# First folded keys in the first dispatch, the second half's statistics first, the last gathers in pairs

## The chip, the cores and the metric

The kernel runs on one core of a Trainium2 chip. The metric is the device time of one execution in microseconds (us), as the median of several runs. TensorE (PE) multiplies matrices from SBUF into PSUM banks, VectorE (DVE) and ScalarE (ACT) work on tiles, GpSimd (POOL) computes and issues indirect DMAs, and SyncE (SP) issues the plain DMAs. Each engine runs its own program in order and waits on semaphores.

## The reference

`x` is [16, 128, 128] in float32, and the context is [16, 77, 96]. Four layers follow each other, and each adds a gated cross-attention to the context and then a gated feed-forward part:

```
layer 0: 16 heads x 8  on the context;  FFN: top 2 of 8 experts, gelu, 128-512-128
layer 1: 16 heads x 64 on the context;  FFN: dense mixture of 8 experts, 128-128
layer 2: 1 head x 128  on the context;  FFN: top 1 of 8 experts, silu, 128-512-128
layer 3: 16 heads x 8  on the context;  FFN: ternary weights, gelu, layernorm
attention: out = softmax(q k^T * scale) v @ Wo
```

In layer 1 the key is `context @ Wk` and the query `x @ Wq`, so the scores of a head are `x (Wq_h Wk_h^T) context^T`. The product in the brackets doesn't depend on the data.

## The kernel before

The program of every engine is written out by hand, with waits on counted semaphores, and goes through the stages in this order: `heads8(0)` (attention of layer 0), `experts(0)`, `heads64` (attention of layer 1), the dense mixture, `head128`, `experts(1)`, `heads8(1)`, the ternary layer. The batches 0 to 15 come in four groups of four (GB = 4), and a group is normalised by `front_a` (statistics, DVE), `rsqrt_front` (POOL) and `front_b` (DVE).

**Experts.** `experts(run)` takes the 2048 tokens in two halves, hh = 2*run and 2*run + 1. For a half, PE transposes (`turn`, L1377) and makes the gate logits (`logits`, L1387), DVE picks the experts (`route`), PE counts (`ranks`, L1396), and DVE computes each token's row (`slots`). POOL scatters the normalised rows to `xs` in DRAM by 16 (top 2) or 8 (top 1) indirect DMAs (`spread`, L701). SP loads them again (L453), and PE works off 23 or 15 tiles per half: `turn_slots` (L1429), up (L1439), and down (L1455). DVE copies each input (`take`, L2206 or L2203) and each output (`give`, L2216), SP stores outputs to `ys` (L502), POOL gathers them (`collect`, L715), and DVE adds them to `x` (`combine`, L2231). The second layer's bias goes to `x` through PE (`second_bias` L1409, `add_bias` L1418) and DVE (`bias8`, L2128). `stats8`, `variance8` (L1993) and `norm8` on DVE, with `token_roots` on POOL between them, normalise a half. `weigh` computes the gate weights. The second half's routing is done in the gap in which the first half's rows go to DRAM and back, and its scatter goes beside the first half's tiles.

**heads64.** `folded_weights` (PE L1505) multiplies Wq and Wk of each head, ACT and DVE split the products into `l1w` high and low parts, and `folded_keys` multiplies them by a group's context, three matmuls for each of 16 heads (L1123 to L1125), with copies to `k1` by ACT and DVE. Before, the products are made inside the second half of `experts(0)`, and the first group's keys at the start of `heads64`. `own_values` makes the values, and `scores` (L1554), exps on ACT (L825) and sums follow batch by batch.

**heads8.** The queries and keys are computed on PE for a group, split, stored to DRAM by SP (`store_queries` L417, `store_keys` L397) and loaded back in another layout (`query_roles` L428, `key_roles` L408). POOL multiplies each batch's keys by a mask (`keys`, L606), and PE makes scores (L1231), exps on ACT, sums (L1265) and products with the values (L1276). In `heads8(1)` SP's order for g = 1, 2, 3 is: for g >= 2 `key_roles(1, g)`, for g = 2 also `store_keys(1, 3)`; `store_queries(1, g)`; `query_roles(1, g)`; and after g = 1 a wait until the feed-forward part of layer 2 has been added to all of `x` ("ff", counted by `combine`), then the loads of the ternary weights (L568 to L570). The gathers and the combination of the very last half, hh = 3, stand in `heads8(1)`: POOL's `collect(3)` at b = 0, DVE's `last_rows` at b = 2.

## Time and profile before

| | us |
|---|---|
| median of 3 runs | 780.34 (780.26 to 781.79) |
| the profiled execution | 786.76 |
| its span in the trace | 784.7 |
| PE busy | 669.0 (85%) |
| DVE busy | 454.6 (58%) |
| ACT busy | 395.8 (50%) |
| POOL busy | 311.4 (40%) |
| mean granted TensorE clock | 0.921 |

The span is the time from the first to the last instruction in the trace. A granted clock of 1.00 is 2.4 GHz, and 0.50 is 1.2 GHz. In the timelines a row has the start, the busy time, the engine and line, the operation and how many instructions it merges; in brackets is the engine's idle time before it, and what ended that. `SPq` is SP issuing a DMA, not the DMA's own time.

### The profile page before, as it was taken

Reading aid. Unit: us, or ns where it says so; the run is one execution under the profiler, and the core shown is the slowest. Engines: PE = TensorE matmul, PEld = TensorE weight load, DVE = VectorE, ACT = ScalarE, POOL = GpSimd, SP = SyncE. Lnnn points to the kernel's source line nnn. Section 1 sums busy time; section 2 is a strip of 40 time slices with the busy share of each in tenths; the row PEclk is TensorE's granted clock in tenths of the full one; section 3 lists DMA queues with packets and bytes.
Section 4 is the critical chain, followed back from the end, with each engine's and each line's share of the span. In section 5 each row is a group of like instructions: output and inputs, shape, how many; then the busy total and the mean of one; then the engine's idle time right before and its main releaser. Section 6 shows DMA issues by size and latency. Waiting matters only on the chain.

```text
span 784.7 us, 17363 instructions
## 1 busy us (share of the span) xinstructions
PE 669.0 (85%) x6445; PEld 557.1 (71%) x6445; DVE 454.6 (58%) x1408; ACT 395.8 (50%) x969; POOL 311.4 (40%) x266
## 2 busy tenths in 40 slices
PE   3799995589999799899998999884699868999894
PEld 3587773379999778688786854563589756777784
DVE  5375768533224668666675667755433334778783
ACT  4475542145566366365665666421155744666471
POOL 4654431725143338123141337502224446545032
PEclk9998998579999999999999999995599987999997
DMA  6543751866775301000000020003357553331001
GB/s 171 153 117 67 209 169 38 257 165 177 230 207 148 88 15 34 1 1 2 1 1 1 2 80 2 1 1 96 110 136 225 162 161 96 115 75 42 3 15 41
DMA packets 60717, 70.93 MB, mean 90 GB/s; under 512 B 7051, under 2 KB 40859, under 8 KB 60635
## 3 DMA queue, kind: packets, MB, share of 16 engines
q1 hardware_dynamic: 57563, 63.52, 28.7%
q0 software_dynamic: 3072, 6.30, 2.7%
q8 instruction: 54, 0.88, 0.5%
q14 instruction: 28, 0.23, 0.1%
HBM read 48.89 MB, written 20.91 MB: 89 GB/s over the span
## 4 chain that ended last, share of the span: by engine, by line
PE 67%; DVE 17%; issue 5%; DMA 4%; ACT 3%; SPq 2%; POOL 1%; POOLq 0%; ACTq 0%; DVEq 0%
PE banks L1439 8%; PE banks L1455 7%; PE banks L1554 4%; PE banks L1276 4%; PE banks L1253 4%; PE banks L1165 3%; PE banks L1563 3%; PE banks L1574 3%; PE banks L1123 3%; PE banks L1231 3%; PE banks L1125 3%; PE banks L1124 3%; PE banks L1265 3%; PE banks L1607 2%; DVE rr L1901 2%
## 5 line engine op out<-in xcount | busy, mean ns | idle before, releaser
L962 ACT ACTIVATE hT<-banks,wup 128x128 f32<-128x128 f32 x304 | 86.5, 368 | 74.4 <-PE banks L1439 60.0
L893 ACT ACTIVATE pT<-banks 77x512 f32<-77x512 f32 x128 | 69.2, 590 | 58.8 <-PE banks L1253 56.8
L1439 PE MATMUL banks<-xTs,wup 128*128 128x128 f32 x608 | 85.0, 286 | 3.2 <-issue 3.2
L701 POOL DMA_INDIRECT xs<-xn,slot x48 | 46.8, 974 | 102.1 <-DVE ysb L2216 52.2
L606 POOL TENSOR_TENSOR kbd<-k,const 96x1248 fp32r<-96x1248 f32 x32 | 72.8, 2285 | 32.6 <-PE banks L1253 30.1
L661 POOL TENSOR_TENSOR sh<-sh,rd 128x616 f32<-128x616 f32 x32 | 38.9, 1216 | 112.1 <-DVE rd L1858 111.8
L1439 PEld LDWEIGHTS banks<-xTs,wup 128*128 128x128 f32 x608 | 78.4, 202 | 4.5 <-issue 4.2
L1455 PE MATMUL banks<-wd,hT 128*128 x608 | 80.8, 277 | 0.3
L2216 DVE COPY ysb<-banks 128x128 f32<-128x128 f32 x76 | 22.1, 291 | 91.9 <-PE banks L1455 82.8
L1455 PEld LDWEIGHTS banks<-wd,hT 128*128 128x128 f32 x608 | 73.8, 192 | 1.1 <-issue 0.8
L586 POOL TENSOR_TENSOR rstd<-vv,const 128x4 f32<-128x4 f32 x24 | 25.4, 1060 | 115.8 <-DVE vv L1805 115.5
L715 POOL DMA_INDIRECT back<-ys,slot x48 | 46.4, 966 | 53.5 <-DMA ys<-ysb 26.8
L1895 DVE TENSOR_REDUCE nm<-banks 128x8 f32<-128x616 f32 x64 | 50.9, 796 | 27.5 <-PE banks L1231 25.2
L825 ACT ACTIVATE sh<-sh 128x308 f32<-128x308 f32 x64 | 27.1, 460 | 43.7 <-DVE sh L1848 42.5
L1901 DVE RECIPROCAL rr<-banks 128x128 f32<-128x128 f32 x32 | 30.6, 956 | 24.2 <-PE banks L1276 24.1
L1253 PEld LDWEIGHTS banks<-q,kbd 128*77 128x77 f32 x448 | 41.6, 156 | 1.9 <-ACT q L800 1.8
L1253 PE MATMUL banks<-q,kbd 128*77 128x128 f32 x448 | 42.3, 240 | 0.6 <-ACT q L800 0.4
L1276 PE MATMUL banks<-pT,vp 128*32 128x128 f32 x1024 | 41.6, 284 | 0.0
L1231 PE MATMUL banks<-kbd,q 96*128 96x312 f32 x112 | 32.6, 375 | 8.4 <-DVE nm L1895 5.7
L1827 DVE SCALAR_TENSOR_TENSOR x<-banks,tg,x 128x128 f32<-128x128 f32 x48 | 16.7, 348 | 38.1 <-PE banks L1574 22.0
L1265 PE MATMUL banks<-pT,const 128*32 128x128 f32 x1024 | 36.3, 280 | 2.2 <-issue 1.5
L800 ACT ACTIVATE prob<-banks 77x512 f32<-77x512 f32 x64 | 33.6, 585 | 8.8 <-PE banks L1165 8.8
(323 smaller groups left out, 1570.7 us busy)
## 6 DMA issues: line engine op xcount, KB each, us to landing
wup<-in_up SPq DMA_DIRECT2D x76, 258.0 KB
q<-queries SPq DMA_DIRECT2D x21, 256.0 KB, 4.3
queries<-qc SPq DMA_DIRECT2D x8, 512.0 KB
wd<-in_down SPq DMA_DIRECT2D x8, 512.0 KB
ys<-ysb SPq DMA_DIRECT2D x16, 256.0 KB
k<-keys SPq DMA_DIRECT2D x24, 156.0 KB, 3.6
xs<-zt SPq DMA_DIRECT2D x2, 1472.0 KB, 10.7
keys<-kc SPq DMA_DIRECT2D x8, 312.0 KB
```

What stands on the lines that cost most here:

```text
L606: pool.tensor_tensor(kbd[b % NB8][0:96, :, :, :].bitcast(F32R), kb, m, ALU.mult).then_inc(h8.kbd, 1)
L701: pool.indirect_dma_start(xs[hh], bass.IndirectOffsetOnAxis(ap=idx[hh % 2][k_][:, t:t + 1], axis=0), xn8[hh % 2][:, t, :], None).then_inc( ...
L715: pool.indirect_dma_start(back[:, k_, t, :], None, ys[hh], bass.IndirectOffsetOnAxis(ap=idx[hh % 2][k_][:, t:t + 1], axis=0))\
L893: act.activation(pT[b % 2][0:SK, u, :], ps[0:SK, 2 + u % 2, :], ACT.Exp, scale=D8 ** -0.5)\
L962: ins = act.activation(hT[T % 3][:, c, :], ps[:, T % 2, c * P:c * P + P], func, bias=wup[T % NW][:, HID + c:HID + c + 1])
L1231: ins = pe.matmul(ps[:, i, 0:HG * SP], q_[0:96, 2 * pair + i, b % GB, :].bitcast(F32R), kbd[b % NB8][0:96, 2 * pair + i, :, :].rearrange(" ...
L1253: ins = pe.matmul(ps[0:SK, 2 + u % 2, j * P:j * P + P], kbd[b % NB8][:, u, j, 0:SK].bitcast(F32R), q_[:, u, b % GB, :].bitcast(F32R), star ...
L1265: pe.matmul(ps[32 * j:32 * j + 32, 4 + b % 2, P:2 * P], const[:, C_PAD + 32 * u:C_PAD + 32 * u + 32], pT[b % 2][:, u, j * P:j * P + P], st ...
L1276: ins = pe.matmul(ps[32 * j:32 * j + 32, 4 + b % 2, 0:P], vp[b // GB % 2][:, at:at + 32], pT[b % 2][:, u, j * P:j * P + P], start=(u == 0) ...
L1439: ins = pe.matmul(ps[:, T % 2, c * P:c * P + P], w_[:, c * P:c * P + P], xTs[T % 3][:, :], start=True, stop=True)
L1455: ins = pe.matmul(ps[:, 6 + T % 2, 0:P], hT[T % 3][:, c, :], wd[:, bass.ds(expert, 1), c * P:c * P + P].rearrange("p o n -> p (o n)"), sta ...
L1895: dve.tensor_reduce(m_, s_, AX.X, ALU.max, negate=True).then_inc(h8.max, 1)
```

## The change

The products of the layer 1 weights and the first group's 16 folded keys are made in the first gap of `experts(0)`. The weights wqT and wkT get a place of their own and are loaded earlier by SP, the keys go to a new tile `k1_first`, and ACT alone copies them. `folded_keys(0, ...)` is gone at the start of `heads64` on PE, ACT and DVE. There PE makes the first four value products right after `front`, and ACT copies them ahead of its first exps. In both runs of `experts` DVE makes the second half's statistics first, PE does `turn` and `logits` ahead of the bias, `bias8(hh, 0)` comes after the second half's routing, and `bias8(hh, 1)` in the first tile. POOL computes `token_roots(1)` after one scatter instead of three, and `token_roots(3)` ahead of the scatters. At the end of the second half of `experts(0)`, `combine`, `front_a` and `front_b` come a tile earlier. In `heads8(1)` `collect(3)` is cut in four pairs of gathers, with the masked keys of batch 3 behind the first, and `last_rows` is cut in two, at b = 2 and b = 5.

```diff
@@ -462,8 +479,6 @@
                     resident(6, 8)
-                    sp.dma_start(wqT[:, :, :], a["wqT"]).then_inc(ld.l1raw, 16)
-                    sp.dma_start(wkT, a["wkT"]).then_inc(ld.l1raw, 16)
...
@@ -536,6 +551,9 @@
                 query_roles(0, g)
+            sp.wait_ge(ld.xrest, 16)
+            sp.dma_start(wqT[:, :, :], a["wqT"]).then_inc(ld.xrest, 16)
+            sp.dma_start(wkT[:, :, :], a["wkT"]).then_inc(ld.xrest, 16)
...
@@ -624,7 +642,7 @@
                 for b in range(B):
-                    if b + 2 < B and (b or run == 0):
+                    if b + 2 < B and (b >= 2 or run == 0):
...
@@ -633,7 +651,11 @@
                         if run:
-                            collect(3)
+                            collect(3, 0, 4)
+                            keys(1, 3)
+                            collect(3, 1, 4)
+                    if run and b in (2, 3):
+                        collect(3, b, 4)
...
@@ -690,8 +712,8 @@
                         m = k_ * HT + t
-                        if hh % 2 == 0 and m == 3:
-                            token_roots(hh + 1)
+                        if hh == 0 and m == 1:
+                            token_roots(1)
...
@@ -764,6 +786,7 @@
             token_roots(2)
+            token_roots(3)
...
@@ -827,6 +850,8 @@
                         outputs(G, i - 2)
+                    if i == 0 and G == 0:
+                        value_copies(0, 0)
...
@@ -951,6 +976,18 @@
+            def folded_weights_hi():
+                for j in range(4):
+                    act.wait_ge(h64.qmm, j // 2 + 1)
+                    copy(folded(0, j), ps[0:DC, 4 * (j // 2) + j % 2, :].rearrange("p (c d) -> p c d", c=4)).then_inc(su.hi, 1)
+            def first_keys():
+                for h in range(H):
+                    act.wait_ge(h64.kmm, h + 1)
+                    copy(k1_first[:, h, :, :].rearrange("p b t -> p (b t)"), ps[:, first_bank(h), 0:GB * SP]).then_inc(h64.q, 1)
...
@@ -965,17 +1002,17 @@
                     tanh(2)
+                else:
+                    folded_weights_hi()
...
                 turned(2 * run + 1, 1)
+                if run == 0:
+                    first_keys()
...
                         hidden(BASE[hh] + i)
-                        if hh == 1 and i in (5, 6, 12, 13):
-                            j = (5, 6, 12, 13).index(i)
-                            act.wait_ge(h64.qmm, j // 2 + 1)
-                            copy(folded(0, j), ps[0:DC, 2 + j % 2, :].rearrange("p (c d) -> p c d", c=4)).then_inc(su.hi, 1)
...
@@ -996,13 +1033,19 @@
-                def own_values(g, part):
+                def value_copies(g, part):
...
                              ps[0:SK, 2 + i % 4, :]).then_inc(h64.v, 1)
+                def own_values(g, part):
+                    if g or part:
+                        value_copies(g, part)
...
@@ -1012,14 +1055,12 @@
-                folded_keys(0, 0)
-                folded_keys(0, 1)
...
                 for g in range(0, NG - 1):
-                    attend(h64, g, D64 ** -0.5, outputs, own_values)
+                    attend(h64, g, D64 ** -0.5, outputs, own_values, value_copies)
...
                 gate_exp(0)
-                attend(h64, NG - 1, D64 ** -0.5, outputs, own_values)
+                attend(h64, NG - 1, D64 ** -0.5, outputs, own_values, value_copies)
...
@@ -1458,12 +1499,21 @@
                 hh = 2 * run
-                second_bias(hh)
-                add_bias(hh)
+                if run == 0:
+                    folded_weights(0)
+                    folded_weights(1)
...
                 logits(hh + 1)
+                second_bias(hh)
+                if run == 0:
+                    first_keys(range(0, 8))
                 ranks(hh + 1)
+                if run == 0:
+                    first_keys(range(8, H))
+                add_bias(hh)
+                if run == 0:
+                    pe.wait_ge(h64.q, H)
...
@@ -1488,21 +1538,25 @@
                             add_bias(hh + 1)
-                        if hh == 1 and i in (3, 10):
-                            folded_weights(i // 10)
...
+            def first_keys(units):
+                ct = tuple(c_[0:DC, 0:GB, :].rearrange("p b t -> p (b t)") for c_ in (chi, clo))
+                pe.wait_ge(su.lo, 2 * NG)
+                for h in units:
+                    if h >= 4:
+                        pe.wait_ge(h64.q, h - 3)
+                    split3(ps[:, first_bank(h), 0:GB * SP],
+                           tuple(w_[0:DC, h // 8, (h % 8) * P:(h % 8) * P + P] for w_ in l1w), ct).then_inc(h64.kmm, 1)
...
-                pe.wait_ge(ld.l1raw, 64)
-                if j == 0:
-                    pe.wait_ge(mo.xb, 4)
-                else:
-                    pe.wait_ge(su.lo, NG + 2)
+                pe.wait_ge(ld.xrest, 48)
...
                     at = h % 8 // 2 * P
-                    ins = pe.matmul(ps[0:DC, 2 + h % 2, at:at + P], wkT[rows, h // 2, :], wqT[rows, h // 2, :],
+                    ins = pe.matmul(ps[0:DC, 4 * j + h % 2, at:at + P], wkT[rows, h // 2, :], wqT[rows, h // 2, :],
...
@@ -1515,24 +1569,31 @@
                     for h in range(8 * part, 8 * part + 8):
-                        if h % 8 >= 4:
-                            pe.wait_ge(h64.q if h % 2 else h64.k, 8 * g + h // 2 - 1)
-                        elif g:
+                        if h % 8 >= 4 and h % 2:
+                            pe.wait_ge(h64.q, by_act(g, h // 2 - 1))
+                        elif h % 8 >= 4:
+                            pe.wait_ge(h64.k, by_dve(g, h // 2 - 1))
+                        else:
                             pe.wait_ge(h64.v, 8 * g - 7 + 4 * part + h % 8)
-                        elif part:
-                            pe.wait_ge(h64.q if h % 2 else h64.k, h // 2 - 1)
...
-                def own_values(g, part):
+                def value_units(g, part):
...
                     for i in range(4 * part, 4 * part + 4):
-                        if i >= 4 and g < NG - 1:
-                            pe.wait_ge(h64.q if i % 2 else h64.k, 8 * (g + 1) + i // 2 + 1)
+                        if i >= 4 and g < NG - 1 and i % 2:
+                            pe.wait_ge(h64.q, by_act(g + 1, i // 2 + 1))
+                        elif i >= 4 and g < NG - 1:
+                            pe.wait_ge(h64.k, by_dve(g + 1, i // 2 + 1))
...
                                tuple(w_[0:DC, 2, 512 * (i % 2):512 * (i % 2) + 512] for w_ in l1w)).then_inc(h64.vmm, 1)
+                def own_values(g, part):
+                    if g or part:
+                        value_units(g, part)
...
@@ -1540,19 +1601,19 @@
                     if b == 0 and u == 0:
-                        pe.wait_ge(h64.k, 8 * g + 8)
-                        pe.wait_ge(h64.q, 8 * g + 8)
+                        pe.wait_ge(h64.k, by_dve(g, 8))
+                        pe.wait_ge(h64.q, by_act(g, 8 if g else H))
...
                         if g < NG - 1:
-                            pe.wait_ge(h64.k, 8 * g + 16)
-                            pe.wait_ge(h64.q, 8 * g + 16)
+                            pe.wait_ge(h64.k, by_dve(g + 1, 8))
+                            pe.wait_ge(h64.q, by_act(g + 1, 8))
...
                     return pe.matmul(ps[:, u % 2, 0:4 * SP].rearrange("p (h t) -> p h t", h=4),
-                                     xT[(g + 2 * NG) % 2][:, b * P:b * P + P], k1[g % 2][:, 4 * u:4 * u + 4, b, :],
+                                     xT[(g + 2 * NG) % 2][:, b * P:b * P + P], folded_rows(g)[:, 4 * u:4 * u + 4, b, :],
...
@@ -1568,15 +1629,14 @@
                 def project(g, b):
-                    pe.wait_ge(ld.l1raw, 96)
+                    pe.wait_ge(ld.l1raw, 64)
...
-                folded_keys(0, 0)
-                folded_keys(0, 1)
                 front(2 * NG)
+                value_units(0, 0)
...
@@ -1942,7 +2002,10 @@
                     if b == 2 and between:
-                        between()
+                        between((0,), (0,))
+                        lk.wait()
+                    if b == 5 and between:
+                        between((0,), (1,))
...
@@ -2177,21 +2240,26 @@
                 hh = 2 * run
+                wait_done(dve, "h1" if run else "h8", 1)
+                stats8(hh + 1, 0)
+                stats8(hh + 1, 1)
+                variance8(hh + 1)
...
                     slots(hh)
-                wait_done(dve, "h1" if run else "h8", 1)
-                stats8(hh + 1, 0)
-                stats8(hh + 1, 1)
-                variance8(hh + 1)
-                weigh(hh, gate)
-                bias8(hh, 0)
+                else:
+                    weigh(hh, gate)
...
                 norm8(hh + 1, 1)
-                bias8(hh, 1)
+                if run:
+                    weigh(hh, gate)
+                if run == 0:
+                    for j in range(4):
+                        folded_weights_lo(j)
...
                     route(hh + 1, part)
+                bias8(hh, 0)
...
@@ -2248,6 +2316,7 @@
                             if i == 0:
+                                bias8(hh, 1)
...
@@ -2256,18 +2325,16 @@
                                 combine(hh - 1, 0, i - 10)
-                            if run == 0 and i in (7, 8, 14, 15):
-                                folded_weights_lo((7, 8, 14, 15).index(i))
-                            if run == 0 and i in (19, 20):
-                                combine(hh - 1, 1, i - 19)
+                            if run == 0 and i in (18, 19):
+                                combine(hh - 1, 1, i - 18)
...
                                 key_lo(1, i - 3)
-                            if run == 0 and i == nt - 2:
+                            if run == 0 and i == nt - 3:
...
                                 front_a(0, n)
-                            if run == 0 and i == nt - 1:
+                            if run == 0 and i == nt - 2:
...
```

## Rows read from the trace of the kernel before

**Rows 1.** The page: which engine's work the chain that ended last was.

```profile
PE 67%; DVE 17%; issue 5%; DMA 4%; ACT 3%; SPq 2%; POOL 1%; POOLq 0%; ACTq 0%; DVEq 0%
```

**Rows 2.** Windows: stretch, length, busy PE, PEld, DVE, ACT, POOL, clock, DMA share, GB/s.

```profile
160.00:166.00 6.00, 5.30 (x24) 4.90 (x25) 1.09 (x4) 1.82 (x7) 0.00 (x0) 0.51 0.81 210
...
265.00:270.00 5.00, 5.00 (x27) 5.00 (x26) 1.93 (x4) 1.55 (x4) 3.54 (x5) 0.68 0.31 105
```

**Rows 3.** Timeline of POOL at the first dispatch: start, us, work, idle before.

```profile
132.90 1.24 POOL L701 DMA_INDIRECT xs<-xn,slot  x1 [23.43 <-DVE slot L2109]
...
155.42 0.96 POOL L701 DMA_INDIRECT xs<-xn,slot  x1 [0.30 <-issue]
```

**Rows 4.** Timeline of PE at the first dispatch and the first tiles.

```profile
160.53 0.69 PE L1429 MATMUL banks<-const,xsb 128*128 128x128 f32 x2 [4.67 <-DMA xsb<-xs]
...
161.66 3.62 PE L1439 MATMUL banks<-xTs,wup 128*128 128x128 f32 x16
...
169.35 1.13 PE L1439 MATMUL banks<-xTs,wup 128*128 128x128 f32 x8
```

**Rows 5.** Timeline of DVE at the first dispatch and the first tiles.

```profile
135.45 0.17 DVE L1993 TENSOR_REDUCE vv<-mv 128x8 f32<-128x16 f32 x1
...
168.96 0.28 DVE L2206 COPY xTs<-banks 128x128 f32<-128x128 f32 x1
...
179.59 1.27 DVE L2128 TENSOR_TENSOR x<-x,banks 128x512 f32<-128x512 f32 x2
```

**Rows 6.** Windows of line 1505 alone: stretch, length, PE, PEld, clock, DMA, GB/s.

```profile
215.00:259.00 44.00, 2.23 (x32) 1.80 (x32) 1.00 0.59 170
```

**Rows 7.** Timeline of PE at the start of heads64.

```profile
260.57 0.41 PE L1123 MATMUL banks<-chi,l1w_hi 96*128 96x312 f32 x1 [1.42 <-DVE ysb L2216]
...
271.25 0.60 PE L1134 MATMUL banks<-const,xn 128*128 128x128 f32 x4
272.62 1.29 PE L1554 MATMUL banks<-k,xT_even 128*128 128x312 f32 x4 [0.78 <-ACT xT_even L800]
```

**Rows 8.** Timelines of SP, ACT and POOL around the start of heads64.

```profile
214.92 0.38 SPq L502 DMA_DIRECT2D ys<-ysb  x1
...
218.70 0.98 POOL L715 DMA_INDIRECT back<-ys,slot  x1 [17.60 <-DMA ys<-ysb]
...
248.27 12.63 SPq L502 DMA_DIRECT2D ys<-ysb  x3
...
272.50 1.28 ACT L825 ACT_TABLE_LOAD   x1
```

**Rows 9.** Timeline of PE at the second dispatch (experts(1)).

```profile
549.50 3.77 PE L1418 MATMUL banks<-b2m,cT 32*128 32x512 f32 x4 [0.51 <-DVE cT L2122]
...
555.95 3.58 PE L1387 MATMUL banks<-rraw,xT 128*128 128x8 f32 x16 [0.78 <-ACT xT L800]
...
566.48 0.47 PE L1429 MATMUL banks<-const,xsb 128*128 128x128 f32 x1 [2.65 <-DVE xTs L2203]
```

**Rows 10.** Chain that ended last, at the start of heads8(1): start, us, what.

```profile
635.10 3.85 DMA queries<-qc
...
639.85 4.97 DMA q_first<-queries
```

**Rows 11.** Timelines of DVE, SP and PE in heads8(1).

```profile
666.94 2.18 DVE L2231 SCALAR_TENSOR_TENSOR x<-back,share,x 128x128 f32<-128x128 f32 x8
...
673.91 0.36 SPq L568 DMA_DIRECT2D wfr<-in_fc  x1
...
676.74 0.38 SPq L397 DMA_DIRECT2D keys<-kc  x1
...
680.59 0.34 SPq L417 DMA_DIRECT2D queries<-qc  x1
...
685.79 0.96 DVE L1901 RECIPROCAL rr<-banks 128x128 f32<-128x128 f32 x1 [1.19 <-PE banks L1276]
...
691.24 0.50 PE L1231 MATMUL banks<-kbd,q 96*128 96x312 f32 x2
```

27 lines of the change are left out of this document (16 added, 11 removed).

## The prediction

> **What bounds the kernel now.** I first read the chain of work that ended last. PE holds 67% of it [rows 1], so anything that only lightens DVE, ACT or POOL is worth nothing, and a gap of PE is worth its full length. Then I followed PE's timeline to the places that the diff touches and looked for the wait that ends last. There are five. At the first dispatch PE waits 4.67 us for the first rows from DRAM, and its first 16 up products take 3.62 us, while 8 of them take 1.13 us later [rows 4]: the granted clock is 0.51 in that stretch [rows 2]. The second half of `experts(0)` is tile after tile of PE work, with the weights' products in it [rows 6]. At the start of `heads64` PE makes keys from 260.57 to 271.25, with only a little else to do [rows 7]. At the second dispatch the first up product waits for DVE, which is still in the second half's `slots` [rows 9]. In `heads8(1)` PE is fed by queries that go to DRAM and back [rows 10, 11].
>
> **1. The first keys leave heads64.** PE's last output is copied out at about 260.5, and `front` starts at 271.25 [rows 7]; the 10.7 us between are 16 keys. All of it goes if nothing else is late. Two things are. `front_b` now comes before DVE's last `give` and PE's transposes start about 1.0 us later than the keys did. The value copies now stand on ACT ahead of the first exps and wait until the last outputs have landed in `ys`: SP ends issuing them at 248.27 + 12.63 = 260.9 [rows 8]. An earlier output store was issued at 214.92, and the gather that waited for it began at 218.70 [rows 8], so about 3.8 us; that gives some 264.7 and with issue gaps 265.6. Then come the copies and a table load of 1.28 us [rows 8]. Old first scores at 272.62 become 262.9 or so, but the first exps are held for about 1.2 us more. I take **-8.5** (bounds -7, both waits in full, and -10.7, none). The copies also fill the idle time of ACT, so they cost nothing later.
>
> **2. Products out of the second half.** 16 products of two forms took 2.23 us of PE at full clock [rows 6], and that stretch has no PE gap that they could have filled: **-2.2**. The same work in the gap of the first dispatch has 4.67 us of idle PE and more before it [rows 4].
>
> **3. The chain to the first rows (run 0).** The first load waits for POOL's 16 scatters, which run back to back from 132.90 to 156.38 [rows 3]. `token_roots(1)` moves from before the fourth to before the second scatter. POOL gets there at 134.14, but its input is written by DVE until 135.62 [rows 5]. Every later scatter is behind this wait in POOL's order: 135.62 - 134.14, with a semaphore's way, **+1.6**. Its bounds: 0, if DVE's earlier statistics (they no longer wait behind anything but the last addition to `x`) come sooner; +3, if PE instead sets the end. PE now has 48 key products before `turn_slots`: the 16 keys took 10.7 us at the start of `heads64` [rows 7], where the clock was at 0.68 for part of the way [rows 2], so I take 12.5 us as the most at the low clock throughout; with turns, logits, counts and a bias product of 3.8 us [rows 9] PE would be ready at about 163.4 against 160.53 [rows 4]. In the first half of the gap PE has work without a pause, and I expect it done by 162.
>
> **4. bias8(0, 1) in the first tile.** Its two halves of DVE work take 1.27 us in another tile [rows 5]. In tile 0 DVE's copy at 168.96 to 169.24 is what PE's product at 169.35 waits for [rows 4, 5], so there is no slack: **+1.3**. In run 1 the same happens: **+1.3**. What hid it before was the gap.
>
> **5. The second dispatch.** Before: bias product 549.50 to 553.27, turns, logits to 559.5, route, ranks, `slots`, take, up [rows 9]; the end is DVE's. Now the statistics are there before `slots(2)` ends, and turns and logits come ahead of the bias product: its 3.77 us and some 3 us of statistics and weights go out of the way, logits end at about 552.6 and `slots(3)`, which ended about 6.6 us behind them, at 559.2. Then PE is the last: ranks at 555.9, bias product to 560.3, `turn_slots`, take and up at 561.2 instead of 566.95. `token_roots(3)` is ahead of the scatters now (POOL was idle there), so the rows are there by 558.6. **-5.7** (bounds -4 and -6.5).
>
> **6. heads8(1), b = 2.** `combine` takes 2.18 us for eight additions [rows 11], and PE waited for the DVE work behind it. Half of it goes to b = 5, where DVE has 1.19 us of idle time [rows 11]: **-1.1**.
>
> **7. heads8(1), SP.** "ff" now means b = 5 of DVE: the work ahead of the new half ends at 685.79 - 1.19 = 684.60 [rows 11], minus the 1.1 of part 6, plus the 1.1 of the half itself, so 684.6. SP waits there in its order for g = 1, and behind it are three loads of ternary weights, `key_roles(1, 2)` (three), `store_keys(1, 3)` and then `store_queries(1, 2)`, which before was issued at 680.59 [rows 11], when its data came. Issuing these (seven, without the last) took from 673.91 to 677.12 before, 3.2 us [rows 11], so the store goes at about 687.95. A store and a load in sequence took 3.85 + 0.9 + 4.97 = 9.7 us at the start of the stage [rows 10], and I allow for 0.8 us less. So the queries of batch 8 are there at 696.7 to 697.7; PE needs them at 691.24 - 1.1 = 690.1 [rows 11]. That is a gap of 6.6 to 7.6 us, and PE comes out of it at a low clock as at the first dispatch [rows 2], for 1.5 to 2 us; some 0.8 us of small DVE waits of that stretch are absorbed. **+8** (bounds +4, if only part of the load is waited for, and +9).
>
> What the change moves at the end of `experts(0)` (`combine`, `front_a`, `front_b` a tile earlier) costs nothing: DVE has idle time before every output copy, and if that were gone it would cost up to 1.1 us, one combination.
>
> **Sum.** -8.5 - 2.2 + 1.6 + 1.3 - 5.7 + 1.3 - 1.1 + 8 = -5.3 us, on a span of 784.7 us in an execution of 786.76 us. The median of the runs shown is 780.34; the profiled one is 0.8% longer, and I take the difference over as it is: **775.0 us**.
>
> **What the Trainium skill adds.** The low clock at the first tiles is shown by the rows. Its page "TensorE: Matmul & The Clock Gate", section "What's actually happening", says that "the default state is throttled, and activity releases the throttle". By that the key products in the gap would be of use twice: the first 16 up products would take about 1.8 us instead of 3.62, and that is rival B. Its page "DMA: Bandwidth & Descriptors", section "Rules for kernel authors", tells the author to issue a DMA early and to wait late. Part 7 does the reverse with SP, and by the fit of the page's section "Anatomy of one DMA — SWDGE (gpsimd) path", 2.0 us plus the bytes by 436 GB/s, an estimate of store and load is 4 + 2.9 = 6.9 us for 0.5 and 0.77 MB. By that the term 7 would be about 2.5 us smaller. The rows have 9.7 for the two [rows 10], and I go by them.
>
> **Rivals.**
> A (forecast): **775.0**, within 771.5 to 778. Chance 0.45.
> B: the gap's key products keep PE busy and the tiles start at the full clock. For it: the clock fell only where PE idled. Against it: PE idles 4.67 us for the rows anyway. The first 16 and next 8 products would be some 2.5 us shorter, and a `heads8(1)` gap of only 4 us (a store right behind "ff") would give 4 more: 775.0 - 2.5 - 4 = **768.5**, or either one, to 772. Chance 0.25.
> D: the wait at the start of `heads64` takes the place of the one removed. ACT stands still for the last `ys` store with the exps queued behind it, and DVE and PE wait for the exps. The first exps were at 273.8 and would be at 269 or later: -4.5 instead of -8.5, **779.0** (778 to 780). For it: SP issued those stores until 260.9 [rows 8], when PE was through with the tiles. Chance 0.17.
> C, slower than before: the SP wait is dearer. Place: from "ff" to the first scores of batch 8. The query store stands behind six loads of weights and keys, and all share the DMA engines; the store and load could take 14 us instead of 9.3, and the batches after the gap run at half the clock for the 5.5 us that the first tiles needed [rows 2, 4], 2.7 us more. Price +16 instead of +8: **783.0**. It decides from a delay of 15 us on, since the other terms sum to -13.3. For it: nothing else on SP can go around the wait. Against: these loads are small. Masked keys on POOL, now queued behind the gathers, would add to it if they became late. Chance 0.13.
> That the change doesn't do what it says (keys in the gap push `turn_slots` out by as much as they save) is inside the +3 of part 3, since 160.53 to 163.4 is much less than 10.7.
>
> **How the numbers follow.** The forecast is that of A. The range of 768.5 to 780.0 leaves out C and a little of B's end. About 0.2%, 1.6 us, is what a measurement of this kernel can tell from no change: faster is at or under 778.8, with A, B and a third of D, 0.76; within 0.2% is the rest of D, 0.11; slower is C, 0.13.
>
> **What would show it.** Right: no L1123 products after the last tile; first scores near 263 and exps before 270; first up product of run 0 near 162 and of run 1 near 561; `store_queries` of group 2 near 688 less the shift, with a gap of PE of 6 to 8 us before the first scores of batch 8. Wrong: a first up product of run 0 after 165 (PE bound), a DVE gap behind the value copies of over 4 us, or no gap of PE at batch 8, which alone would make it 767.

## The result and the profile after

The changed kernel takes **776.63 us** (median of 20 runs, 773.57 to 783.96), the kernel before 780.51 (20 runs, 778.23 to 783.11). The ratio is 0.9958 [0.9939, 0.9977]: 0.42% faster, 3.3 us (3.9 us by the medians; the interval is 1.8 to 4.8). The forecast was 775.0 in a range of 768.5 to 780.0. The profiled execution took 774.30 us with a span of 772.1, 2.3 below its median, while the profiled one of before was 6.3 above the median of 780.51. So the two traces differ by 12.6 us, and most of what that has over 3.3 is a difference of executions. I therefore read stages, each against traces of other kernels that have the same code in that stage. The traces start at different offsets, so times are compared from one milestone to the next, and not as they stand.

The page's chain, to hold against [rows 1]:

```profile
PE 65%; DVE 17%; DMA 6%; issue 4%; ACT 3%; POOL 3%; SPq 1%; POOLq 0%; ACTq 0%; DVEq 0%
```

DMA and POOL have gained on the chain, PE has lost. The four places follow, each as the timeline of one engine. First PE at the first dispatch:

```profile
153.85 1.98 PE L1459 MATMUL banks<-b2m,cT 32*128 32x512 f32 x4
160.02 0.66 PE L1470 MATMUL banks<-const,xsb 128*128 128x128 f32 x2 [4.19 <-DMA xsb<-xs]
161.12 3.62 PE L1480 MATMUL banks<-xTs,wup 128*128 128x128 f32 x16
170.45 1.13 PE L1480 MATMUL banks<-xTs,wup 128*128 128x128 f32 x8 [1.03 <-issue]
```

The keys are in the gap and PE still waits 4.19 us for the first rows (4.67 in [rows 4]); the 16 up products still take 3.62 us. The windows of PE show why (stretch, length, PE busy, clock, DMA share, GB/s):

```profile
149.00:156.00 7.00, 6.64 (x36) 0.99 0.15 49
156.00:160.00 4.00, 0.00 (x0) 0.50 0.45 103
160.00:164.00 4.00, 3.81 (x17) 0.50 0.95 277
```

The granted clock was 0.99 while PE worked and 0.50 after it had stopped. It was also 0.50 in the windows 144 to 146 and 146 to 148, with PE busy with keys for all of the 4 us: these keys were themselves made at half the clock. POOL, which sends the rows, has a new wait ahead of its second scatter (`token_roots`, L629), and the last of the 16 scatters starts 24.23 us after the first, 22.52 in the kernel before [rows 3]:

```profile
130.57 1.24 POOL L723 DMA_INDIRECT xs<-xn,slot  x1 [23.41 <-DVE slot L2172]
133.38 1.67 POOL L629 TENSOR_TENSOR rstd<-vv,const 128x8 f32<-128x8 f32 x1 [1.57 <-DVE vv L2056]
...
154.80 0.96 POOL L723 DMA_INDIRECT xs<-xn,slot  x1 [0.30 <-issue]
```

At PE's fourth tile there is a new wait of 1.03 us, and DVE's timeline has what held it: `bias8(0, 1)` and, behind it, the gate weights of `weigh` (seven small operations, of which the first is shown) ahead of the copy that PE needs:

```profile
167.67 1.27 DVE L2191 TENSOR_TENSOR x<-x,banks 128x512 f32<-128x512 f32 x2
168.86 0.16 DVE L2112 TENSOR_SCALAR rs<-rs 128x8 f32<-128x8 f32 x1
...
170.07 0.28 DVE L2274 COPY xTs<-banks 128x128 f32<-128x128 f32 x1
```

Next the start of `heads64`, PE, then ACT:

```profile
259.21 0.66 PE L1175 MATMUL banks<-const,xn 128*128 128x128 f32 x4 [1.58 <-DVE ysb L2284]
262.50 1.22 PE L1615 MATMUL banks<-k_first,xT_even 128*128 128x312 f32 x4
```

```profile
261.35 2.04 ACT L823 ACTIVATE v<-banks 77x512 f32<-77x512 f32 x4 [0.84 <-DMA ys<-ysb]
263.41 1.28 ACT L848 ACT_TABLE_LOAD   x1
264.70 0.81 ACT L848 ACTIVATE sh<-sh 128x308 f32<-128x308 f32 x2
```

No key product stands between the last output copy and `front` (10.7 us in [rows 7]). The wait for `ys` is there, but costs ACT 0.84 us, and the table load runs beside the DVE subtraction (L1908, from 264.14) whose result the exps need anyway: the first exps start at 264.70, 2.20 us behind the first scores. In the kernel before they stood 2.23 us behind them, and waited for that subtraction, not for the table load, which ended at 273.78:

```profile
274.85 0.85 ACT L825 ACTIVATE sh<-sh 128x308 f32<-128x308 f32 x2 [1.07 <-DVE sh L1848]
```

At the second dispatch, PE (to hold against [rows 9]):

```profile
545.33 3.78 PE L1459 MATMUL banks<-b2m,cT 32*128 32x512 f32 x4
...
550.22 3.62 PE L1480 MATMUL banks<-xTs,wup 128*128 128x128 f32 x16
```

The bias product is now the last thing before the tiles, and nothing is waited for behind it. Last `heads8(1)`: DVE's half combination, SP and PE:

```profile
662.37 1.13 DVE L2299 SCALAR_TENSOR_TENSOR x<-back,share,x 128x128 f32<-128x128 f32 x4
```

```profile
663.53 0.36 SPq L586 DMA_DIRECT2D wfr<-in_fc  x1
...
664.94 2.31 SPq L425 DMA_DIRECT2D k<-keys  x3
...
667.83 0.38 SPq L434 DMA_DIRECT2D queries<-qc  x1
```

```profile
678.10 0.89 PE L1272 MATMUL banks<-kbd,q 96*128 96x312 f32 x2 [8.84 <-DMA q<-queries]
```

The second half of the additions ends at 663.50 and SP goes on at 663.53: the wait of part 7 of the forecast. The query store stands six DMAs behind it, and PE idles 8.84 us for what it brings. The page's chain goes through exactly these loads, with 4.25 us for the store's DMA and 5.06 for the load behind it (3.85 and 4.97 in [rows 10]).

### The profile page after: what moved, and what is told of

Its sections match the earlier page's. It is cut to its first block, busy times and chain, and to the rows that moved or that the text cites. A ratio compares the mean times of both kernels' runs of the same rounds, so it can differ in the third digit from the quotient of the medians.

```text
span 772.1 us, 17362 instructions
## 1 busy us (share of the span) xinstructions
PE 665.8 (86%) x6445; PEld 557.5 (72%) x6445; DVE 452.2 (59%) x1400; ACT 399.3 (52%) x977; POOL 312.1 (40%) x266
## 4 chain that ended last, share of the span: by engine, by line
PE 65%; DVE 17%; DMA 6%; issue 4%; ACT 3%; POOL 3%; SPq 1%; POOLq 0%; ACTq 0%; DVEq 0%
PE banks L1480 9%; PE banks L1496 7%; PE banks L1615 4%; PE banks L1294 3%; PE banks L1317 3%; PE banks L1206 3%; PE banks L1624 3%; PE banks L1635 3%; PE banks L1272 3%; PE banks L1164 3%; PE banks L1165 3%; PE banks L1166 2%; PE banks L1306 2%; PE banks L1667 2%; DVE rr L1961 2%
## 6 DMA issues: line engine op xcount, KB each, us to landing
xs<-zt SPq DMA_DIRECT2D x2, 1472.0 KB, 12.6
```

## The stages of every kernel

Below is the time between milestones of PE's timeline, in us: the last row of scores of `heads8(0)` to the first transposed rows (**dispatch**), to the end of the tiles of run 0, to the first scores of `heads64` (**start**), to `head128`'s last product with `b_raw`, its last queries (**attention**), to the first up product of run 1 (**dispatch 2**), to the end of its tiles (**tiles 2**). The stretch from there to the first scores of `heads8(1)` is left out (8.3 to 9.8 us). **End** goes from those scores to PE's last product, and 9.9 us follow it in every trace.

| | dispatch | tiles | start | attention | dispatch 2 | tiles 2 | end |
|---|---|---|---|---|---|---|---|
| before | 42.91 | 98.63 | 13.46 | 243.68 | 50.45 | 69.66 | 129.65 |
| after | 44.73 | 97.62 | 4.86 | 242.41 | 45.31 | 69.29 | 134.36 |
| e1_sp_late | 44.90 | 97.10 | 6.30 | 242.38 | 44.03 | 70.52 | 126.32 |
| e3_after_no_pairs | 44.52 | 97.69 | 4.73 | 242.49 | 45.32 | 71.30 | 127.33 |
| e2_before_pairs_split | 42.97 | 97.48 | 13.39 | 243.60 | 50.37 | 68.80 | 137.87 |
| e4_before_split | 42.80 | 97.68 | 13.38 | 243.67 | 50.11 | 67.91 | 135.59 |
| e5_before_keys3_first | 43.03 | 97.91 | 13.41 | 243.54 | 49.92 | 68.01 | 131.16 |
| e8_after_run1_old | 45.72 | 98.00 | 4.73 | 242.51 | 49.76 | 68.13 | 136.40 |
| e6_bias_gap | 44.78 | 95.81 | 4.85 | 240.81 | 44.54 | 67.75 | 125.68 |
| e7_warm | 44.45 | 94.81 | 4.61 | 242.34 | 45.26 | 67.68 | 127.79 |
| e12_keys_11 | 44.73 | 97.04 | 6.28 | 242.49 | 44.07 | 66.92 | 126.39 |
| e9_roots_m3 | 48.11 | 98.41 | 4.71 | 242.35 | 45.32 | 69.32 | 130.53 |
| e10_roots_warm | 53.42 | 96.00 | 4.68 | 242.45 | 44.19 | 68.73 | 132.03 |
| e11_keys_again | 48.28 | 98.75 | 13.12 | 241.40 | 44.44 | 68.84 | 130.29 |

Up to `heads8(1)` the code of before stands in four traces (before, e2, e4, e5) and that of after in three (after, e1, e3). Among them dispatch and attention repeat to within 0.4 us; start and dispatch 2 differ by up to 1.6 and 1.3 us, tiles 2 by 2.0. In the start of e1 and e12 the four value products of PE ran at half the clock (0.50 and 0.55 in the windows from 260 to 262, 1.00 in the changed kernel), and this is their 1.5 us. So one trace is enough for terms of several us, and for none of one. The trace of e6 is of an execution 4.7 us under its median, the fastest of six.

## The experiments

**SP's order in heads8(1), from the changed kernel.** The theory was that the loss of 8 us comes from the wait alone: put it and the ternary loads behind the queries of g = 2.

```diff
 # e1_sp_late
-                if g == 1:
+                if g == 2:
...
-                    if run and b in (6, 10, 11, 12, 14):
-                        ternary_weights((6, 10, 11, 12, 14).index(b))
+                    if run and b in (7, 10, 11, 12, 14):
+                        ternary_weights((7, 10, 11, 12, 14).index(b))
```

> The changed kernel, but SP waits for ff and loads the ternary weights only after the queries of group 2 (store_queries(1, 2), query_roles(1, 2)), and DVE's first ternary step moves from b = 6 to b = 7. Theory (SP's order makes the 8.84 us gap of PE before batch 8): the gap is gone, with the low clock after it, the span is 8 to 10 us shorter than that of the changed kernel, about 768 us, 0.984 of before. Rival (the late ff costs the time wherever it stands: the ternary loads are then late for DVE and POOL at b = 6 and 7): the gap only moves one or two batches on, and the time stays within 3 us of the changed kernel, 774 to 777.

Measured: 768.38 us, ratio 0.9844 [0.9819, 0.9869]: 8.2 us under the changed kernel by the medians, 8.9 by the ratios (1.14%). The stage end is 8.0 shorter. SP, and PE's scores of batch 8:

```profile
660.44 0.34 SPq L434 DMA_DIRECT2D queries<-qc  x1
...
667.54 0.36 SPq L586 DMA_DIRECT2D wfr<-in_fc  x1
```

```profile
672.90 0.50 PE L1272 MATMUL banks<-kbd,q 96*128 96x312 f32 x2
```

The store goes before the ternary loads, the scores of batch 8 wait for nothing, and in PE's stretch from 668 to 676 (669 to 678 is the gap of the changed kernel) 6.90 of 8.00 us are busy at a clock of 1.00. Beside SP's wait and the loads behind it only DVE's first ternary step moved, by one batch, since it reads what they load: the place of the wait is the cause.

**The same edits in the kernel before.** If that is so, the later half of the last combination alone must make the kernel before slower. e4 cuts `last_rows` in two; e2 also has the gathers in pairs.

```diff
 # e4_before_split
-                        between()
+                        between((0,), (0,))
+                        lk.wait()
+                    if b == 5 and between:
+                        between((0,), (1,))
 # e2_before_pairs_split: as e4, and
-                    if b + 2 < B and (b or run == 0):
+                    if b + 2 < B and (b >= 2 or run == 0):
...
-                            collect(3)
+                            collect(3, 0, 4)
+                            keys(1, 3)
+                            collect(3, 1, 4)
+                    if run and b in (2, 3):
+                        collect(3, b, 4)
```

> The kernel before with the edits in heads8(1) alone: gathers in pairs, keys(1, 3) behind the first pair, last_rows at b = 2 and b = 5. Theory: batches 0 to 3 gain about 4 us and the gap before batch 8 costs 8 to 9, so about 4.5 us slower than before, 785 us, 1.006. Rival (the edits are a gain, and the gap seen in the changed kernel's trace comes from its other parts): 776 to 777 us, 0.995.

> The kernel before with one edit: the last combination cut in two, at b = 2 and b = 5, gathers as before. Theory: the gap before batch 8 alone, +8 to +9, less 1.1 for the half that leaves b = 2: 787 to 788 us, 1.009. Rival (the gap needs the pairs too, since their last gathers make ff late): within 1.5 us of before.

Measured: e4 789.38, ratio 1.0106 [1.0083, 1.0129]; e2 790.25, 1.0124 [1.0099, 1.0149]. PE in e4:

```profile
691.31 0.89 PE L1231 MATMUL banks<-kbd,q 96*128 96x312 f32 x2 [8.66 <-DMA q<-queries]
```

The gap of the changed kernel stands there (8.83 us in e2), and the split alone brings it: +8.3 us against the 781.04 of the kernel before, measured beside it, and +9.2 with the pairs, with intervals that overlap. For e4 I had expected 787 to 788, for e2 785, which was too low: the gain of 4 us in the first batches didn't come.

**The changed kernel without them.** e3 has `collect(3)`, the masked keys and `last_rows` as before, and all else changed.

```diff
 # e3_after_no_pairs
-                            collect(3, 0, 4)
-                            keys(1, 3)
-                            collect(3, 1, 4)
-                    if run and b in (2, 3):
-                        collect(3, b, 4)
+                            collect(3)
...
-                        between((0,), (0,))
-                        lk.wait()
-                    if b == 5 and between:
-                        between((0,), (1,))
+                        between()
```

> The changed kernel with heads8(1) as before: eight gathers in a row, last_rows whole at b = 2. Theory: 4.5 us faster than the changed kernel, about 772 us, 0.989 of before, and no gap of PE before batch 8. Rival (pairs help): 3 to 4 us slower than the changed kernel, 780 us.

Measured: 769.86 us, ratio 0.9854 [0.983, 0.9878]. The parts outside `heads8(1)` are worth 11.4 us (1.46% of 780.51), and those inside cost 0.9958 / 0.9854 = +1.06%, 8.2 us, with some 2.4 us of uncertainty from the two intervals. I had expected 4.5 us for them.

**Masked keys ahead of the gathers.** One piece of the change seemed harmless or good: POOL makes batch 3's keys before most gathers.

```diff
 # e5_before_keys3_first
-                    if b + 2 < B and (b or run == 0):
+                    if b + 2 < B and (b >= 2 or run == 0):
...
-                            collect(3)
+                            collect(3, 0, 4)
+                            keys(1, 3)
+                            for part in range(1, 4):
+                                collect(3, part, 4)
```

> The kernel before with one edit: in heads8(1) the masked keys of batch 3 come behind the first two gathers instead of behind all eight; the combination stays whole at b = 2. Theory: PE's wait for these keys goes (0.71 us in the trace of e4_before_split), 0.5 to 1 us of gain, time within 0.2% of before. Rival (the gathers ahead of the keys are what made the start of heads8(1) 3.8 us longer in the trace of before than in that of the changed kernel): 3 to 4 us faster, 0.995.

Measured: 784.64, ratio 1.0048 [1.0025, 1.007], some 3.8 us slower; theory and rival were both wrong. POOL, then DVE:

```profile
651.56 2.26 POOL L606 TENSOR_TENSOR kbd<-k,const 96x1248 fp32r<-96x1248 f32 x1 [3.84 <-PE banks L1256]
...
660.26 0.94 POOL L718 DMA_INDIRECT back<-ys,slot  x1 [0.30 <-issue]
661.22 1.29 POOL L622 TENSOR_TENSOR x<-x,a_raw 128x512 f32<-128x512 f32 x1
662.45 2.27 POOL L606 TENSOR_TENSOR kbd<-k,const 96x1248 fp32r<-96x1248 f32 x1
```

```profile
660.67 6.05 DVE L2234 SCALAR_TENSOR_TENSOR x<-back,share,x 128x128 f32<-128x128 f32 x8
```

The keys wait 3.84 us for PE and push the six gathers behind them. The last one is issued at 660.26, and the eight additions then fall beside two POOL products of 1.29 and 2.27 us: they take 6.05 us instead of 2.18 [rows 11]. PE's next scores came after 1.99 us of idle time. The excess of 3.87 us on DVE is of the size of the 3.8, but no run removes the overlap alone, so this cause is argued and not shown.

**The tile-0 stall.** e6 is e1 with `bias8(0, 1)` and the gate weights in the gap of run 0, and `weigh` a tile later in run 1.

```diff
 # e6_bias_gap: as e1, and after slots(hh + 1)
+                if run == 0:
+                    bias8(hh, 1)
+                    weigh(hh + 1, gate)
...
-                            if i == 0:
+                            if i == 0 and run:
                                 bias8(hh, 1)
+                            if i == 1 and run:
```

> e1_sp_late with the bias additions and the weights of the second half moved out of tile 0: in run 0 into DVE's idle time behind slots(1), in run 1 the weights from tile 0 to tile 1. Theory (term 4: 1.3 us in each run, and the weights' share of the stall too): up product of the fourth tile 8.8 us or less behind the first transposes in run 0, and 1 to 1.5 us sooner in run 1, 2 to 3 us in all, 766 us. Rival (DVE's stall in tile 0 is made up by later tiles, which wait for ACT and loads anyway): no gain.

Measured: 765.48, ratio 0.9813 [0.9777, 0.9848]. The totals of e6 and e1 can't be told apart by their intervals, so the expected gain of 2 to 3 us isn't shown; the stage can be told apart. PE in e6, the first transposes and the fourth tile:

```profile
160.91 0.66 PE L1470 MATMUL banks<-const,xsb 128*128 128x128 f32 x2 [4.25 <-DMA xsb<-xs]
...
169.56 1.06 PE L1480 MATMUL banks<-xTs,wup 128*128 128x128 f32 x8
```

That is 8.65 us from the one to the other, 8.82 in the kernel before [rows 4], and 160.02 to 170.45, 10.43, in the changed kernel. The wait of 1.02 to 1.03 us at the fourth tile stands in all four traces with that code (the changed kernel, e1, e3, e8) and in none of those without it (e6, e7, e12).

**Rival B by itself: PE kept busy.** e7 is e6 with transposes that nobody reads, 32 in the first gap, 12 and 8 around the turns of the second.

```diff
 # e7_warm: as e6, and
+                def warm(n):
+                    for _ in range(n):
+                        pe.transpose(ps[:, 0, 0:P], idn, idn)
...
+                else:
+                    warm(12)
...
+                else:
+                    warm(8)
...
+                    warm(32)
```

> e6_bias_gap with transposes of a constant that nobody reads, in PE's waits: 32 in run 0 between the bias product and the first rows, and 12 and 8 in run 1 around the logits. Theory (the first tiles are slow only because PE idled before them): granted clock near 1.00 from the first tile on in run 0, its first 16 up products in 1.8 us instead of 3.62, 2 to 2.5 us less in run 0, and 0 to 3 less in run 1. Rival (the clock comes up too late whatever PE did before, or the first rows and weights bound these tiles): 3.62 us again and no gain, or a loss by the transposes that run late.

Measured: 764.87, ratio 0.9802 [0.9769, 0.9836]. PE and its windows in run 0:

```profile
156.99 3.71 PE L1449 MATMUL banks<-const 128*128 128x128 f32 x32
161.27 0.44 PE L1475 MATMUL banks<-const,xsb 128*128 128x128 f32 x2 [0.56 <-DMA xsb<-xs]
162.15 1.96 PE L1485 MATMUL banks<-xTs,wup 128*128 128x128 f32 x16
```

```profile
156.00:160.00 4.00, 4.00 (x31) 1.00 0.18 56
160.00:164.00 4.00, 3.16 (x27) 1.00 0.91 255
```

With the gap filled the clock is 1.00 and the 16 products take 1.96 us instead of 3.62. The tiles are 1.0 us shorter than e6's; in the whole time that isn't measurable. Run 1 stayed at 3.62, so the 20 fillers there gave nothing.

**The second dispatch.** e8 has run 1's order on DVE and PE, and `token_roots(3)`, as before.

```diff
 # e8_after_run1_old (core)
+                if run:
+                    second_bias(hh)
+                    add_bias(hh)
...
+                if run:
+                    for part in range(4):
+                        route(hh, part)
+                    slots(hh)
```

> The changed kernel with the order of the second dispatch as before (statistics behind slots(2), bias products ahead of the turns and logits, bias additions ahead of the tiles, token_roots(3) among the scatters). Theory: the first up product of run 1 comes 5.7 us later and tile 0 is 1.3 us shorter, so 4 to 4.5 us slower than the changed kernel, 781 us, 1.001 of before. Rival (the gain was run-to-run variation of the profiles): within 1.5 us of the changed kernel.

Measured: 780.8, ratio 1.0007 [0.9981, 1.0033], beside 0.9958 for the changed kernel. The stage is back at 49.76 us, and the first up product waits for DVE as in [rows 9]:

```profile
557.38 0.48 PE L1471 MATMUL banks<-const,xsb 128*128 128x128 f32 x1 [2.64 <-DVE xTs L2278]
557.65 3.62 PE L1481 MATMUL banks<-xTs,wup 128*128 128x128 f32 x16
```

**POOL's roots late again, and fillers.** e9 is e6 with `token_roots(1)` before the fourth scatter; e10 adds 24 unread transposes to it.

```diff
 # e9_roots_m3: as e6, and
-                        if hh == 0 and m == 1:
+                        if hh == 0 and m == 3:
 # e10_roots_warm: as e9, and after the keys, in run 0
+                    warm(24)
```

> e6_bias_gap with token_roots(1) behind the third scatter again, as in the kernel before. Theory (term 3: POOL waits 1.57 us for the variance, and every scatter behind it is late by that): the first transposes of run 0 come 1.5 to 1.9 us sooner, 43.0 us after the last scores of heads8(0) instead of 44.8, and the span is 1.5 us shorter, 764 us. Rival (the later norm8(1) makes turns, logits and keys late, and PE or DVE then sets the first tile): no gain or a loss of up to 1 us.

> e9_roots_m3 with 24 transposes of a constant, read by nobody, between the bias product and the first rows of run 0 alone. Theory: the first 16 up products take 1.9 to 2.0 us instead of 3.62, as in e7_warm, 1 to 2 us less than e9_roots_m3, 762.5 us. Rival (what the clock gives is taken by the next wait, for DVE's input copies and the weights' loads): within 0.5 us of e9_roots_m3.

Measured: e9 774.27, 0.9855 [0.9817, 0.9892]; e10 777.77, 0.9887 [0.9843, 0.993], both measured beside a kernel before that took 784.55. Both missed. POOL did what e9's theory said: the last scatter starts 22.64 us after the first, as in the kernel before (24.24 in e6). But PE came later. In e9, at the end of the dispatch:

```profile
160.05 3.78 PE L1459 MATMUL banks<-b2m,cT 32*128 32x512 f32 x4
163.76 0.69 PE L1470 MATMUL banks<-const,xsb 128*128 128x128 f32 x2
```

The bias product that ended at 155.8 in the changed kernel ends at 163.8, at half the clock, and the transposes follow it with no wait: the rows are no longer what comes last. Ahead of it ACT and DVE stood still together, and PE idled 2.83 us before 156.03 (one row of each of the two):

```profile
155.54 0.43 ACT L823 ACTIVATE k_first<-banks 128x312 f32<-128x312 f32 x1 [3.09 <-remote]
```

```profile
156.28 0.23 DVE L2153 TENSOR_TENSOR plan<-banks,const 128x64 f32<-128x64 f32 x1 [4.94 <-remote]
```

With PE as the bound, e10's fillers delay the tiles by their full length, and in this execution they began at the low clock, 24 of them in 5.38 us where e7 had 32 in 3.71:

```profile
164.48 5.38 PE L1449 MATMUL banks<-const 128*128 128x128 f32 x24
```

Behind them the first 16 up products took 1.95 us instead of 3.62, as the theory said, and the tiles 96.00 instead of 98.41: 2.4 us back for 5.3 us paid. So these two say nothing, by their times, on what the earlier `token_roots` costs.

**The keys put back.** e11 is e6 with 48 unread key products before `front` of `heads64`, on PE alone.

```diff
 # e11_keys_again: as e6, and in heads64
+                for h in range(H):
+                    split3(ps[:, 2 + h % 2, 0:GB * SP],
+                           tuple(w_[0:DC, h // 8, (h % 8) * P:(h % 8) * P + P] for w_ in l1w), ct)
```

> e6_bias_gap with 48 matmuls of the size of the first keys put again at the start of heads64 on PE, ahead of front; nobody reads them and nobody copies them. Theory (PE's work between the last tile and the first scores sets that stretch, term 1): 48 by 0.143 us is 6.9 us, less 1.5 us in which PE waited there anyway, so the first scores come 5.4 us later and the time is 5 to 7 us up, 771 us. Rival (the copies of the keys by ACT and DVE, or the wait for the last stores, made the old stretch long): under 2 us.

Measured: 782.75, beside e9 and e10, 0.9972 [0.9949, 0.9996]. Against its own base e6 (0.9813, measured at another time) that is +1.6%, 12.4 us, with 3.5 us of it in the dispatch, which was PE-bound in this trace; against e9, whose dispatch was so too, it is +1.2% by the ratios, 8.5 us by the medians. The start stretch is 13.12 us, that of before (13.4), with neither ACT nor DVE given back their copies. The keys begin only after the last output copy:

```profile
264.33 0.41 PE L1164 MATMUL banks<-chi,l1w_hi 96*128 96x312 f32 x1 [1.41 <-DVE ysb L2291]
```

PE's products alone are enough to make the whole stretch. I had expected 5.4 us, and it is 8.3 (13.12 against 4.85 in e6). Of the difference 1.5 us is the idle time before `front`, which I had counted as cover: PE has to wait for that output first, so nothing was covered. The rest is the clock: the 48 products took 8.48 us and not 6.9, with 0.79 and 0.78 granted in the windows from 264 to 272.

**More keys ahead of ranks.** e12 is e6 with 11 keys instead of 8 before `ranks`, so that PE is done earlier.

```diff
 # e12_keys_11: as e6, and
-                    first_keys(range(0, 8))
+                    first_keys(range(0, 11))
...
-                    first_keys(range(8, H))
+                    first_keys(range(11, H))
```

> e6_bias_gap with 11 instead of 8 of the first keys ahead of PE's ranks, so that PE doesn't idle for the 0.7 to 1.5 us in which it waited for DVE's choice there. Theory (that idle time, at 148.9 to 150.4, is what lets the clock fall again within the gap in some executions, and with a clock of 0.50 the keys, the bias product and nothing else set the first tile, 48 us behind the last scores of heads8(0) instead of 44.8): the clock stays at 1.00 from 150 to the bias product, the first transposes come 44.8 us behind, and the executions lie closer together than those of e6_bias_gap, at 0.978 to 0.981 of before. Rival (the low clock is the result of pauses of ACT and DVE in the gap, 3 to 5 us long in the trace of e9_roots_m3, not their cause): ratios of 0.981 to 0.986 with the same spread, and 45 to 48 us again where such a pause falls into the gap.

Measured: 765.12, ratio 0.9822 [0.9797, 0.9847]. The ratio lies in the rival's 0.981 to 0.986, just outside the theory's 0.978 to 0.981, but its interval reaches into both; the runs spread over 5.6 us (e6: 7.0), and the dispatch is e6's (44.73). Inconclusive.

## Why the prediction was right, step by step

The sign, the range and the mechanism held: two blocks of opposite sign, each some three times the net. The time lies well inside the range, and the terms came out near their forecasts one by one, so little of it is luck. Between the two profiled executions themselves 4.71 us go against the 12.6 in the end stage, and 2.3 of the 12.6 fall before the first milestone, where only SP's loads of wqT and wkT are new: that is a difference of executions. The terms, in us (means of the four old and three new traces; the last row but one by the times of e3):

| part | forecast | measured |
|---|---|---|
| 1 first keys out of heads64 | -8.5 (-7 to -10.7) | start -8.1; attention -1.2 |
| 3 dispatch, run 0 | +1.6 | +1.8 |
| 2 and 4, tiles of run 0 | -2.2 + 1.3 | -0.5 |
| 5 second dispatch | -5.7 | -5.3 |
| 4 tiles of run 1 | +1.3 | +1.8, in 67.9 to 71.3 |
| 6 and 7, heads8(1) | -1.1 + 8 | +8.2 (by e3, ±2.4) |
| all | -5.3 | -3.3 |

**Part 1** held, with two pieces off. The wait for the last `ys` is 0.84 us on ACT: SP ended issuing those stores at 259.54 (245.81 + 13.73), and ACT went on at 261.35, 1.8 us later and not 3.8. And the table load lies beside DVE's subtraction, so the exps are not held by 1.2 us; the forecast had read the end of the table load, 273.8, as the old first exps, which start at 274.85. The attention stretch became 1.2 us shorter in all three traces, which I had put at nothing. Part of it can be where the milestone stands, though no run separates it: the first four value products (2.87 us of PE, 259.63 to 262.50) came behind the first scores before, and now come ahead of them, in the start. So start and attention belong together: -9.3 against the -8.5 of the forecast. Rival D, the wait that takes the place of the keys, didn't occur: the first exps stand 7.1 us behind the last tile, 15.7 us before. What the keys cost is borne out by e11.

**Part 2** can't be separated from part 4. **Part 4** was short by a term: not only `bias8` but also `weigh` came into DVE's way in tile 0, so that the fourth tile was 10.43 - 8.82 = 1.6 us later instead of 1.3. In e6, without both, it is at 8.65.

**Part 3** was right in size, and the traces show its mechanism: POOL waits 1.57 us for DVE's variance, the last scatter starts 1.7 us later behind the first (24.23 against 22.52), and the first transposes follow it by as much as before (5.22 us, 5.11). In e9 that wait and that delay are gone; what it would have given in time isn't shown, since PE set the end there. The upper bound, PE at the low clock, is real but was too small: 163.4 in the time of the kernel before is a dispatch of 45.8 us, and it was 48.11 in e9 and 48.28 in e11, 5.2 and 5.4 us over the old one instead of 3. The forecast had it as a bound, but not as something that comes and goes from run to run. It may be why the changed kernel spreads over 773.6 to 784.0 and the one before over 778.2 to 783.1; no trace of one of its longer executions is there to show that.

**Rival B** failed for the reason that its text gave against it: PE idles 4.19 us anyway and the clock is 0.50 after that. It is a true price, 3.62 - 1.96 = 1.66 us, that only unread work collected in full (e7, and e10 with 1.95). The Trainium skill, "TensorE: Matmul & The Clock Gate", section "What's actually happening", has the same rule (throttled by default, activity releases), and e7 agrees.

**Part 5** held within 0.4 us, by the order described: bias product last, tiles at once. (The forecast took the old first up product to be at 566.95, where the transposes ahead of it end; it starts at 566.75.) e8 confirms it on both the stage (49.76) and the total.

**Part 7** had the gap itself too short: it is 8.84 us and not 6.6 to 7.6. Its cost of +8 was near all the same, since e1, which takes the wait alone away, gives 8.2 to 8.9. From the additions' end to the store 3.35 us were foreseen, and it was 667.83 - 663.50 = 4.33, since three key loads took 2.31 us to issue, and 1.31 in the kernel before; from the store to the scores 10.27 us (8.9 to 9.7 foreseen). Then come some 4 us at the low clock, in the windows of PE:

```profile
669.00:678.00 9.00, 0.26 (x4) 0.64 0.75 201
678.00:680.00 2.00, 1.91 (x14) 0.50 0.49 96
680.00:682.00 2.00, 2.00 (x34) 0.58 0.03 8
682.00:685.00 3.00, 3.00 (x50) 1.00 0.00 0
```

Parts 6 and 7 together are +8.2 by e3, where I had +6.9. Rival C, +16, stayed far off. "DMA: Bandwidth & Descriptors", section "Rules for kernel authors", of the Trainium skill says to issue a DMA early and to wait for it late; e1 is that rule applied, for 8.2 us. The forecast's estimate of 6.9 us for store and load, by the fit in that page's section "Anatomy of one DMA — SWDGE (gpsimd) path", is under the 4.25 + 5.06 = 9.31 us of the two DMAs here, which SP issued and not GpSimd. **Part 6** was not seen apart: e1 keeps the divided combination and e3 doesn't, and their ratios (0.9844 and 0.9854) have overlapping intervals.

The net: the forecast -5.3 and the measured -3.3 differ by 2.0 us. By the table 1.3 of these are parts 6 and 7, and the rest is about 0.8: e3's 11.4 against the 12.2 that the other parts summed to. Both are smaller than the uncertainty of these sums, so this split is a reading and not shown.

**What would beat both kernels.** e1, e6, e7 and e12, all with SP's wait one group later, have ratios of 0.9844, 0.9813, 0.9802 and 0.9822; their intervals overlap, so no order among them is shown.

## What to carry to other kernels

When a counted event gets a later meaning, look up every engine that waits on it, and list what stands behind that wait in the engine's own order: here one line of SP's program ate over two thirds of the gain, and moving it one group on brought that back. A step moved into a gap is worth its full length only if the gap's owner, here the rows from DRAM, still comes last, so compute the time at which the moved work ends at the low clock too. Judge a small net by its blocks, each built alone, and not by two traces whose executions differ by more than the change is worth.

## What was unexpected in the hardware

**A DVE operation waited for a POOL one.** In e1 the half combination took 3.14 us, and in the changed kernel 1.13; the rows of e1, DVE and POOL:

```profile
664.37 3.14 DVE L2299 SCALAR_TENSOR_TENSOR x<-back,share,x 128x128 f32<-128x128 f32 x4
```

```profile
664.31 2.27 POOL L624 TENSOR_TENSOR kbd<-k,const 96x1248 fp32r<-96x1248 f32 x1 [1.24 <-PE banks L1294]
```

The excess of 2.0 us is about what was left of the POOL product, 2.2; in the changed kernel POOL had nothing beside the additions. In e5 it is 3.87 us for POOL products of 3.56. A copy of 128x512 (`lnb`), 0.43 us in the kernel before, took 2.37 us in the changed one beside a POOL product of 2.29. The Trainium skill, "SBUF — State Buffer", section "🔬 SBUF: two separate sides", says that DVE and GpSimd share one pair of ports that one of them holds for a whole instruction while the other is fully blocked, among other cases for a DVE instruction with two SBUF inputs beside a GpSimd one that reads SBUF. The additions are such instructions, and these durations agree. e1 beat the changed kernel with this stall in it.

**ACT and DVE pause.** In e9 both stood still for 3 to 5 us with the releaser given as "remote", and PE idled 2.83 us in that time. Nothing in the traces explains it, and it is left open.

**Fillers cost by the clock at which they start.** The same transpose took 0.116 us each in e7 (3.71 / 32), where the clock was 1.00, and 0.224 us in e10 (5.38 / 24), where it was low at their start. In e7 they stood in a wait for the rows and cost nothing measurable; in e10 PE was what ended last, and the dispatch grew by their whole length.
